# Linear attention: the next half's layer norm before the score products, a landing buffer for its transpose, two banks for the state

## The reference, cut to what matters

```python
x = x + attn_a(layernorm(x)); x = x + ffn(layernorm(x))
h = layernorm(x)                                   # (x - mean) / sqrt(var + 1e-5)
q, k, v = phi(h @ W_Q.T), phi(h @ W_K.T), h @ W_V.T # phi(u) = elu(u) + 1
for t in range(T):                                 # per batch and head
    S = g * S + outer(k[t], v[t])
    z = g * z + k[t]
    y[t] = (S.T @ q[t]) / (z @ q[t] + 1e-6)
x = x + (y * sigmoid(h @ W_g.T + b_g)) @ W_O.T
x = x + ffn(layernorm(x))
```

## Time and profile before

| | us |
|---|---|
| three runs | 1882.01, 1883.61, 1888.32 |
| median | 1883.61 |
| profiled execution, on the device | 1885.07 |
| its span, first to last instruction | 1883.3 |
| TensorE busy | 1828.9 (97%) |
| VectorE busy | 1394.4 (74%) |
| ScalarE busy | 880.3 (47%) |
| GpSimd busy | 592.0 (31%) |

### The profile page before, as it was taken

The page is one execution under the profiler, slowest core; times in us unless marked ns, Lnnn a source line. Parts: engine busy times, 40 slices in busy tenths (PEclk is TensorE's granted clock), DMA queues, the critical chain, the costliest instruction groups (busy, mean ns, idle before and its releaser), DMA issues.

```text
span 1883.3 us, 37415 instructions
## 1 busy us (share of the span) xinstructions
PE 1828.9 (97%) x12929; PEld 1529.6 (81%) x12929; DVE 1394.4 (74%) x2679; ACT 880.3 (47%) x1717; POOL 592.0 (31%) x542
## 2 busy tenths in 40 slices
PE   8999999999999999989999999999999999999998
PEld 7888888888888888877777777878787877888887
DVE  6566566556668888778777878787878788888885
ACT  6656656665654444443333333333333332444443
POOL 5313203211332222233433333434343334522211
PEclk9999999999999999999999999999999999999999
DMA  7100000000022122120000000000000001222332
GB/s 246 43 1 0 0 0 0 0 0 0 13 48 59 29 33 31 28 63 13 13 12 12 11 11 11 11 11 11 11 11 11 12 12 22 40 58 63 64 59 54
DMA packets 230631, 53.21 MB, mean 28 GB/s; under 512 B 209696, under 2 KB 228768, under 8 KB 230176
## 3 DMA queue, kind: packets, MB, share of 16 engines
q1 hardware_dynamic: 229296, 49.53, 13.0%
q10 hardware_dynamic: 1264, 2.76, 0.4%
HBM read 18.69 MB, written 8.39 MB: 14 GB/s over the span
## 4 chain that ended last, share of the span: by engine, by line
PE 70%; DVE 14%; issue 7%; POOL 4%; ACT 2%; SPq 1%; DMA 1%; DVEq 0%; ACTq 0%; POOLq 0%
PE PS L1212 16%; PE PS L1221 9%; PE PS L331 8%; PE PS L870 7%; PE PS L841 6%; PE PS L340 5%; PE PS L1750 3%; PE PS L859 3%; PE PS L1729 3%; PE PS L881 2%; PE PS L1679 2%; PE PS L1717 2%; DVE lin_zq L1515 2%; SPq L270 1%; PE PS L1740 1%
## 5 line engine op out<-in xcount | busy, mean ns | idle before, releaser
L331 PE MATMUL PS<-ln_xh,lin_w 128*128 128x512 f32 x768 | 249.9, 394 | 3.8 <-DVE lin_kT L1498 2.7
L1144 ACT ACTIVATE ff_silu<-PS 128x512 f32<-128x512 f32 x192 | 114.4, 597 | 235.5 <-PE PS L1212 207.3
L1179 DVE SCALAR_TENSOR_TENSOR ff_h<-PS,ff_silu 128x512 f32<-128x512 f32 x192 | 131.2, 684 | 113.1 <-PE PS L1212 99.3
L331 PEld LDWEIGHTS PS<-ln_xh,lin_w 128*128 128x128 f32 x768 | 145.2, 189 | 40.5 <-DVE lin_kT L1498 8.7
L577 POOL TENSOR_TENSOR qk<-qk,swapped 64x128 f32<-64x128 f32 (+2 forms) x96 | 96.9, 1010 | 240.1 <-DVE swapped L721 234.3
L1163 DVE TENSOR_TENSOR ff_h_lo<-ff_h,ff_h_hi 128x512 fp32r<-128x512 f32 x192 | 165.0, 860 | 0.4
L870 PE MATMUL PS<-probT,v_a 128*128 128x128 f32 x1152 | 153.3, 278 | 0.0
L870 PEld LDWEIGHTS PS<-probT,v_a 128*128 128x128 f32 x1152 | 139.5, 192 | 14.3 <-ACT probT L641 7.4
L331 PE MATMUL PS<-ln_xl,lin_w 128*128 128x512 f32 x384 | 150.7, 393 | 0.0
L841 PE MATMUL PS<-qk 128*128 128x512 f32 (+3 forms) x384 | 145.2, 489 | 0.9 <-POOL qk L577 0.9
L166 POOL TENSOR_SCALAR ln_var_eps<-ln_mean_var 128x4 f32<-128x4 f32 x64 | 15.5, 242 | 401.9 <-DVE ln_mean_var L139 401.9
(11 more groups left out here) (191 smaller groups left out, 5325.1 us busy)
## 6 DMA issues: line engine op xcount, KB each, us to landing
ff_raw<-ln_xn SPq DMA_DIRECT2D x464, 32.0 KB, 2.0
ln_xl<-ln_xn SPq DMA_DIRECT2D x288, 32.0 KB, 2.0
out_x<-X SPq DMA_DIRECT2D x15, 512.0 KB, 2.9
X<-in_x SPq DMA_DIRECT2D x7, 1024.0 KB, 5.4
stage<-in_w_lin SPq DMA_DIRECT2D x1, 2048.0 KB, 8.4
stage<-in_w_gate SPq DMA_DIRECT2D x2, 768.0 KB, 7.3
stage<-in_w_up SPq DMA_DIRECT2D x2, 768.0 KB, 8.7
stage<-in_w_down SPq DMA_DIRECT2D x2, 768.0 KB, 10.1
```

The source lines that it names most:

```text
L331: last = nc.tensor.matmul(out, w, x, start=n == 0, stop=n == len(terms) - 1)
L1144: nc.scalar.activation(silu[:, f % NB_GU, :], PS[:, f % NB_GU, :], ACT.Silu, scale=W_SCALE).then_inc(silu_done.sem, 1)
L1179: nc.vector.scalar_tensor_tensor(h[:, f % 2, :], PS[:, NB_GU + f % NB_GU, :], W_SCALE, silu[:, f % NB_GU, :], ALU.mult, ALU.mult).then_inc ...
```

## The change

- **Order on VectorE.** The statistics go into items 0 and 1 (two tiles each), their aggregation into item 2. The second multiplication by the queries moves from item 6 behind item 7. Normalising and the block transpose move from behind the reciprocal to directly behind the last `sums_by_query`, that is, ahead of the score products, the scaled keys and the inverse.
- **Landing buffer.** A new SBUF tensor `landing` (4 KB in each partition) takes the 16 DMAs. SyncE no longer waits for the last value item, except for the unit of the following feed-forward layer, which lands in `ln_xl` as before. ScalarE and GpSimd read `landing`. To make room, the scratch for descriptors made in software is set to 8192 bytes.
- **Order on GpSimd.** The two pieces of the low part follow `gated_low` in c = 1 and c = 2, one piece each.
- **State banks.** The state's increment alternates between banks 4 and 5, and `state` has no wait on the former addition any more. `RING` becomes (4, 2, 5, 3).
- **Order on TensorE.** The keys' transposes of chunk c+1 come before the output projection of chunk c-2. This differs only in c = 2 of the first half of a batch, the one place where both are there.

```diff
+        landing = sb("landing", [P, KT, UN])
-        RING = (5, 2, 4, 3)
-        KEY_BANK, OUT_BANK, ST_BANK, DEN_BANK = 6, (2, 3), 4, 7
+        RING = (4, 2, 5, 3)
+        KEY_BANK, OUT_BANK, ST_BANK, DEN_BANK = 6, (2, 3), (4, 5), 7
+        def landing_of(nfront):
+            return landing[:] if nfront is front else None
...
-                    wait_alone(sp, proj_ready.sem, proj_ready.at(b, NITEM * (half + 1)), front.sp_passed)
-                    nfront.sp_move(sp, n, 0)
+                    if nfront is not front:
+                        wait_alone(sp, proj_ready.sem, proj_ready.at(b, NITEM * (half + 1)), front.sp_passed)
+                    nfront.sp_move(sp, n, 0, landing_of(nfront))
...
-                        if c == 2:
-                            nfront.pool_low_part(pool, n, 0, 0)
                         if c > 0:
                             gated_low(b, UT * half + c - 1)
-                        if c == 2:
-                            nfront.pool_low_part(pool, n, 0, 1)
+                        if c in (1, 2):
+                            nfront.pool_low_part(pool, n, 0, c - 1, landing_of(nfront))
...
-                        elif it in (4, 6):
-                            sums_by_query(b, half, it // 2 - 2)
+                        elif it == 4:
+                            sums_by_query(b, half, 0)
                         elif it == 2 * NP - 1:
                             for j in range(NP // 2, NP):
                                 key_sums(b, half, j)
-                            for j in range(NP // 2, NP):
+                            for j in range(1, NP):
                                 sums_by_query(b, half, j)
-                        if it >= UT - 1 and it < 2 * UT - 1:
-                            nln.dve_tile_stats(dve, nturn, [it - (UT - 1)])
+                        if it < 2:
+                            nln.dve_tile_stats(dve, nturn, [2 * it, 2 * it + 1])
+                        if it == 2:
+                            nln.dve_aggregate(dve, nturn)
...
-                    nln.dve_aggregate(dve, nturn)
+                    nln.dve_normalise(dve, nturn)
+                    nfront.dve_blocks(dve, nturn, (front, b * NHALF + half))
                     decayed_scores(b, c0, 0)
                     decayed_scores(b, c0, 1)
                     scaled_keys(b, c0)
                     inverse(b, half)
-                    nln.dve_normalise(dve, nturn)
-                    nfront.dve_blocks(dve, nturn, (front, b * NHALF + half))
...
                 pe.wait_ge(ks_done.sem, ks_done.at(b, ch + 1))
-                pe.wait_ge(s_done.sem, s_done.at(b, ch))
...
                         earlier_values(b, half, c)
+                        if c + 1 < UT and ch + 2 < NC:
+                            keys(b, half, c + 1)
                         if c >= 2:
                             out_projection(b, ch - 2)
-                        if c + 1 < UT and ch + 2 < NC:
-                            keys(b, half, c + 1)
```

More of the change, by code:

```diff
@@ L1483, in turn @@
                             nfront, n = next_of(b, half, last)
-                            nfront.act_high(act, n, 0)
+                            nfront.act_high(act, n, 0, landing_of(nfront))
                 if last:
@@ L1547, in update_state @@
                     old = S[rows, :, cols]
-                    new = PS[rows, ST_BANK, :].rearrange("p (j a) -> p j a", j=NP)[:, :, cols]
+                    new = PS[rows, ST_BANK[c % 2], :].rearrange("p (j a) -> p j a", j=NP)[:, :, cols]
                     if c == 0:
@@ L1739, in state @@
                         at = j * P + r * DK
-                        last = nc.tensor.matmul(PS[r * DK:(r + 1) * DK, ST_BANK, at:at + DK], ks[:, 2 * j + r, :],
+                        last = nc.tensor.matmul(PS[r * DK:(r + 1) * DK, ST_BANK[ch % 2], at:at + DK], ks[:, 2 * j + r, :],
                                                 v[:, c, 2 * j + r, :], start=True, stop=True)
@@ L1884 @@
     }
-    nc = bacc.Bacc("TRN2", target_bir_lowering=False, num_devices=1)
+    nc = bacc.Bacc("TRN2", target_bir_lowering=False, num_devices=1, dynamic_dma_scratch_size=8192)
     io = {}
```

## The result

| | before | after |
|---|---|---|
| median of five runs, us | 1883.61 (1882.01 to 1888.32) | 1863.60 (1862.06 to 1864.51) |
| ratio, 95% interval | 1 | 0.9887 (0.9870 to 0.9904) |
| span of the profiled execution | 1883.3 | 1861.8 |
| its mean granted clock | 0.995 | 0.997 |
| first to last spread of the linear attention (15 halves) | 722.32 | 700.74 |

The kernel became 20.0 us faster; 14.8 were forecast (1869), and the range held the time. The last row of the table is my finest measure from here on: the start of the 16th spread on TensorE less the start of the first, in one profile. Two profiles whose code is the same in those halves gave 700.74 and 700.79. Lines of `kernel.py` have moved by 4 to 6: the spread is L1706, the product by the queries L1528, the output projection L1754, its low part L1439.

What follows compares the result with a forecast made beforehand. TensorE, busy 737.5 of 774 us in the linear attention, was taken as the bound. Terms 8.9 + 9.3 + 1.7 + 1.0 - 3.2 - 0.8 - 2.1 = 14.8 us gave a median of 1869, range 1857 to 1887.

Steps and rivals of the forecast that it cites:

- State banks and transposes: TensorE at the state's increment: waits of 4.9 + 2.5 us and 15 restarts of 0.1 go, 8.9 us gained.
- Landing buffer: Second halves, output projection's wait for GpSimd's low part goes: 9.3 us gained, plus 1.7 of slow clock.
- the new order: VectorE, normalising and block transpose ahead of the inverse: chain from last product to reciprocal's end grows by 2.2 us.
- First half of a batch: Last product 0.64 us earlier, reciprocal 1.6 later against slack 1.85 less 0.1: spread 0.15 earlier in 7 halves, 1.0 gained.
- Second half: Last product 0.1 us earlier, spread 0.4 late: 8 x 0.4 = 3.2 lost, and 0.8 for 8 restarts.
- L169: GpSimd's 1.04 us instruction, now among VectorE's scans and two-SBUF-input products: cost bounded by 0 and 0.9, taken as 0.
- The first rival: L169 holds the port: VectorE stands 0.9 us in 15 halves before the inverse, 13.5 lost, 1882.5; chance 0.20.
- the third: Waits at the spread make TensorE's clock fall in half of 15 halves: 13 us more, about 1895; chance 0.12.
- The second rival: No new meetings of GpSimd's products, which fall beside phi: spread bound by TensorE, 12.4 us more gained, 1856.5; chance 0.16.
- The fourth: The output projection's wait stays at 0.95 because ScalarE's or GpSimd's order still costs it: 9 to 11 us missing, 1880; chance 0.10.
- The very first half: Normalising waits some 2 us for GpSimd's query products, L166 and L169, on top of 2.2: 2.1 us lost.
- The very last half: Keeps its waits; change put at nothing, between -1 and +2 us; more than 2 would make the prediction wrong.

Runs made afterwards that it cites:

- rstd_early: Changed kernel with GpSimd making the next norm's 1/sqrt(variance) ahead of its four query products instead of behind them; 1858.9 us.
- query_behind: Changed kernel with GpSimd's 1/sqrt(variance) first and its four query products held back until the denominators are there; 1848.3 us.
- undo_banks: Changed kernel with one state bank, its wait for the former addition and the old ring; 1865.3 us.
- undo_keys: Changed kernel with the key transposes of c = 2 back behind the output projection, two banks kept; 1864.9 us.
- undo_landing: Changed kernel without the landing buffer: SyncE waits for the last value item, data land in ln_xl; 1873.1 us.
- v1_rstd: rstd_early with the block transpose behind the reciprocal and GpSimd's low pieces in chunk 2, one each side of the gated low part; 1862.0 us.
- query_cast: query_behind with, in the last half alone, GpSimd's first group of weight casts ahead of 1/sqrt(variance); 1845.0 us.
- stats_back: Changed kernel with the next norm's statistics back in items 3 to 6 and their aggregation behind item 7; 1921.1 us.

## Why the prediction was right, and where its steps were not

**State banks and transposes: the sum right, its parts not.** 8.9 forecast, 8.4 between the spreads when both are undone. But with both undone only the wait of 0.61 returns, at 1.0 a half where 0.71 was reckoned; the wait of 0.36, 3.2 of the 8.9 with its restarts, stays away, so something else in the change removed it. That either edit alone does most of the work was not in the text.

**Landing buffer: the sum near, the credit misplaced.** 11.0 were forecast with the clock's share; undone, it costs 7.4 in the profile and 11.7 by the ratio. But the wait for the low part that it was to cure returns with the new order undone, not with the buffer undone. The forecast counted the 7 us by which the blocks are ready earlier as the buffer's, and these come from the new order, which undone costs 6.1 where I had booked it at 3.0 lost. Together the two parts were forecast at 8.0. The three undone parts (8.4, 7.4, 6.1) sum to 21.9, and the whole gain between the spreads is 21.6. No version undoes these two together, and the banks and keys show how far single costs can miss a joint one, so that these two are worth 13 is not shown.

**First half of a batch: right by errors that cancel.** The spread was forecast 0.15 earlier and is 0.14 earlier (29.74 behind the half's first projection, 29.88 before). The step "the last product is 0.64 earlier" was too small: against item 8 it is 1.1. The step "0.1 for the hand-over" was too small as well: reciprocal's end to spread is 0.43. The chain behind the product grew by 2.4, not 2.2. 1.1 - 2.4 + 1.85 - 0.43 = 0.1.

**Second half: right in the same way.** Forecast 0.4 late and 0.1 for the restart, measured 0.56 (29.94 for 29.38). The last product is 0.44 earlier, not 0.1; the chain grew by 2.4 and the hand-over takes 0.43 here as well. 0.44 - 2.4 + 1.85 - 0.43 = -0.5. The text had said that it would be wrong if the last product isn't 0.6 and 0.1 earlier: it is 1.1 and 0.44, so by its own sign this step failed, and that the spread came out right is luck.

**Behind the spread** first halves gained 1.63, where my terms gave 1.17 (0.36 and 0.61 of waits, two restarts), second halves 0.94 (forecast 1.05). In first halves the gaps themselves were 1.07 before and none after; the other 0.56 is matmuls that took longer behind a wait or stood in another order, where I had put 0.2. A steady batch thus gained 2.15 instead of 1.87, which is 2.1 us of the missing 4.7 (21.6 less my 16.9 for these halves); the other 2.6 lie in the first four halves and the 14th, whose excess over a steady half I had not costed beyond the one wait of 1.84 and its clock.

**The wait that I announced wrongly.** The text has TensorE ready 0.9 earlier in a first half and the spread 0.15 earlier, and then announces a wait of 0.1 or less there. By its own numbers it is 0.75; it is 0.88. That slip hid where the next gain lay, in every half and not in second halves alone.

**L169: taken at 0, and 0 it is.** GpSimd's two small instructions in that half, beside the products of the group above:

```profile
1115.36 1.14 POOL L166 TENSOR_SCALAR ln_var_eps<-ln_mean_var 128x4 f32<-128x4 f32 x1
1116.58 1.84 POOL L169 TENSOR_TENSOR ln_rstd<-ln_var_eps,ln_minus_half 128x4 f32<-128x4 f32 x1
```

It starts at 1116.58 and takes 1.84: its 1.04, and 0.8 in which, I read, it stands until the scan has ended at about 1117.5. The product that starts at 1117.67 beside it keeps its 0.69. The first rival falls, and with it the third, which needed its 0.9. The second rival was right in that these meetings were worth some 11 us, and wrong in that the change would avoid them: it took rstd_early and query_behind to do that. The fourth fell: the output projection's wait went in all halves but the last.

**The very first half** lost 0.8, forecast 2.1: the last product ended 0.8 earlier there, which the text had not counted. **The very last half: wrong.** Taken at nothing between -1 and +2, it lost 3.5. VectorE, GpSimd and TensorE there:

```profile
1563.01 2.50 DVE L155 TENSOR_SCALAR ln_xn<-X,ln_mean_var,ln_rstd 128x256 f32<-128x256 f32 x4
...
1563.20 1.35 POOL L288 TENSOR_TENSOR ln_xl<-ln_xl,ln_xh 128x512 fp32r<-128x512 f32 x1
1564.50 2.30 POOL L1427 CAST lin_w<-stage 128x256 fp32r<-128x256 f32 x6
...
1568.85 1.98 PE L1722 MATMUL PS<-lin_AD,lin_v 128*64 128x128 f32 x16 [3.23 <-DVE stage L1565]
```

The stretch from 1568 to 1575, then the same wait in rstd_early and the stretch around it, columns as in the earlier trace rows:

```profile
1568.00:1575.00 7.00, 6.15 (x36) 5.85 (x37) 2.57 (x6) 0.63 (x1) 2.49 (x2) 0.51 0.35 52
```

```profile
1564.10 1.09 PE L1722 MATMUL PS<-lin_AD,lin_v 128*64 128x128 f32 x16 [3.25 <-DVE stage L1565]
...
1563.00:1570.00 7.00, 4.71 (x41) 4.04 (x42) 3.33 (x8) 1.26 (x2) 4.07 (x5) 1.00 0.33 50
```

The loss has two parts. VectorE's four normalising instructions take 2.50 beside GpSimd's low piece and casts, where they took 1.62 in the kernel before, and TensorE waits for the gated product behind them: some 0.8. The other 2.7 are the clock: around the end of the wait of 3.23 it stood at 0.51 for 7 us. That is not the price of the two banks. rstd_early has two banks and the same wait and kept a clock of 1.00 there. Its last two output projections start 25.0 and 30.4 us behind the spread; in undo_banks, with one bank, it is 24.9 and 30.4, in the changed kernel 27.7 and 33.1, in the kernel before 24.2 and 29.6. In undo_keys, undo_landing and query_behind the same wait was followed by about half as long at the lower level. So some 2.7 of the 3.5 hang on how the clock fell in this one execution. The step that failed is "keeps its waits": the term was put at nothing, though the normalise of the next unit met GpSimd there, and though two banks let TensorE run on into one wait of 3.23 (in the kernel before the longest was 2.19), around which the clock fell in five of the six profiles that have it. The text had called itself wrong if this half changed by more than 2 us, and by that sign too it failed.

**The 3.2 us before the linear attention** are chance by the other profiles; in the total they all but cancel the last half's 3.5.

## What to carry to other kernels

Two edits that break the same chain of waits at different links must be undone together before their worth is known: singly they cost 1.0 and 1.4 us, together 8.4. Before work is moved off a shared resource, ask where the partner could stand instead: holding four GpSimd products back until VectorE had only single-input work gave, with the roots ahead of them, another 11 us between the spreads, half of what the whole change had given. And do not set a transfer to arrive just in time by its length in a steady pass; in the first passes it was up to 2.3 us longer (12.70 in v1_rstd for 10.4).

## What the runs showed of the hardware

- A GpSimd instruction on 4 elements per partition (L169) does not hold VectorE up for its 1.04 us (the product beside it keeps 0.69), while it takes 1.84 itself when a scan is under way. GpSimd products on 512 elements and VectorE's scan lengthen each other: 1.71 for 1.21, and 1.75 for 1.26. The Trainium skill (SBUF — State Buffer, Who interferes with whom) says that whoever issues first has the shared pair of ports for the whole instruction. With L169 the trace does not agree, and the measurement decides.
- In the fourteen profiles, between the first spread and the last output projection, TensorE's granted clock fell only at waits of 1.69 us (v1_rstd) or more, and never at the waits of 0.9 before the spread. Longer ones went both ways. It fell after 1.84 and stayed after 1.85 (query_cast); it fell after 2.87 (0.79 over 8 us) in most halves of stats_back and stayed in three; it fell after 3.23 (0.51 over 7 us) and stayed after 3.25 (rstd_early). 1.00 is the level of 2.4 GHz, and 0.51 all but wholly that of 1.2.
- Sixteen DMAs of 32 KB took 10.4 us on SyncE's queue in every steady half, and 10.71 to 12.70 where a packet of the queues marked "instruction" came before the last of them was issued.
